# Loads, constants and expert tables moved away from the head of a five-stage kernel

## The reference

```
h = window attention 8x8, 8 heads, rotary positions, on x, then a projection
h = h + local attention over a 7x7 neighbourhood, 8 heads
h = h + feed-forward: relu(Wi h + bi); 2 layers of (shared + one of 16 routed experts + h); Wo
h = h + retention: (q k^T / 8) * 0.99^(i-j) for i >= j, times v, no softmax
h = h + binary experts: sign(x) @ sign(sum of gated weights) * scale, 8 gates
```

## Time and profile before

| | us |
|---|---|
| median of 3 runs | 2014.37 |
| the profiled execution's own time | 2015.21 |
| its span | 2013.4 |
| TensorE busy in the span | 1750.3 (87%) |
| VectorE busy | 1180.1 (59%) |
| ScalarE busy | 973.5 (48%) |
| GpSimd busy | 413.1 (21%) |
| mean granted clock of TensorE | 0.958 |

### The profile page before, as it was taken

The page is one execution under the profiler, slowest core; times in us unless marked ns, Lnnn a source line. Parts: engine busy times, 40 slices in busy tenths (PEclk is TensorE's granted clock), DMA queues, the critical chain, the costliest instruction groups (busy, mean ns, idle before and its releaser), DMA issues.

```text
span 2013.4 us, 94727 instructions
## 1 busy us (share of the span) xinstructions
PE 1750.3 (87%) x35818; PEld 1295.4 (64%) x35818; DVE 1180.1 (59%) x3383; ACT 973.5 (48%) x1765; POOL 413.1 (21%) x474
## 2 busy tenths in 40 slices
PE   1899999966758888888888779999999999999997
PEld 0566666644547777767777557777777777777774
DVE  1456666657724444444444467777777777777762
ACT  0334444423312222222222227777777777777776
POOL 2000000024413233332333222222212222222210
PEclk9799999979878999999999879999999999999998
DMA  3000000114433333434334212333333333333332
GB/s 119 13 12 10 13 13 10 34 33 99 98 89 90 97 97 92 98 96 97 96 93 97 64 37 76 77 77 77 77 78 77 76 78 78 78 78 78 78 77 56
DMA packets 254030, 141.69 MB, mean 70 GB/s; under 512 B 181170, under 2 KB 217906, under 8 KB 253714
## 3 DMA queue, kind: packets, MB, share of 16 engines
q1 hardware_dynamic: 253970, 140.85, 28.3%
HBM read 63.53 MB, written 18.42 MB: 41 GB/s over the span
## 4 chain that ended last, share of the span: by engine, by line
PE 48%; issue 30%; SPq 13%; DVE 4%; ACT 2%; POOL 1%; DMA 1%; DVEq 0%; POOLq 0%; ACTq 0%
PE ps_D L783 12%; PE ps_AV L797 5%; SPq L395 5%; PE ps_D L708 4%; DVE m_sb L1216 2%; SPq L366 2%; PE ps_OT L903 2%; PE ps_J L885 2%; PE ps_OT L866 2%; PE ps_J L830 2%; PE ps_D L704 2%; PE ps_J L857 2%; PE ps_T L876 2%; PE ps_J L911 1%; SPq L384 1%
## 5 line engine op out<-in xcount | busy, mean ns | idle before, releaser
L1035 ACT ACTIVATE prob<-ps_D 128x1024 bf16<-128x1024 f32 x448 | 443.0, 1020 | 98.6 <-PE ps_D L783 98.1
L1216 DVE TENSOR_REDUCE m_sb<-ps_D 128x4 f32<-128x400 f32 x256 | 135.3, 570 | 197.8 <-PE ps_D L686 181.6
L1023 ACT ACTIVATE prob<-ps_D 100x512 f32<-100x512 f32 x256 | 138.8, 594 | 218.4 <-PE ps_D L708 218.4
L474 POOL TENSOR_TENSOR tile_a<-q_st,q_mask 128x1024 f32<-128x1024 f32 x64 | 123.3, 1926 | 400.0 <-DMA q_st<-q_d 348.8
L708 PE MATMUL ps_D<-tile_a,key_patch 64*100 64x128 f32 x2048 | 177.9, 289 | 0.0
L704 PE MATMUL ps_D<-mT,key_rows 64*100 64x128 bf16 x1024 | 129.8, 225 | 51.0 <-ACT mT L1012 32.2
L1170 DVE TENSOR_REDUCE top<-ps_D 128x8 f32<-128x512 f32 x128 | 79.5, 683 | 142.2 <-PE ps_D L562 142.2
L783 PE MATMUL ps_D<-tile_b,w_parts 128*128 128x256 bf16 x1024 | 156.4, 276 | 3.2 <-ACT prob L1035 1.3
L783 PE MATMUL ps_D<-tile_a,w_parts 128*128 128x256 bf16 x1024 | 154.0, 273 | 5.0 <-DVE xg L1315 2.5
L797 PE MATMUL ps_AV<-prob,lane_sum 128*32 128x256 bf16 x2048 | 150.6, 284 | 1.5 <-ACT prob L1035 1.5
L708 PEld LDWEIGHTS ps_D<-tile_a,key_patch 64*100 64x100 f32 x2048 | 147.7, 167 | 0.0
(11 more groups left out here) (172 smaller groups left out, 3911.8 us busy)
## 6 DMA issues: line engine op xcount, KB each, us to landing
tile_b<-v_d SPq DMA_DIRECT2D x640, 40.0 KB
tile_a<-xg SPq DMA_DIRECT2D x384, 64.0 KB, 2.0
tile_b<-xg SPq DMA_DIRECT2D x384, 64.0 KB, 2.0
key_st<-k_d SPq DMA_DIRECT2D x64, 175.0 KB, 3.0
key_st<-k_d SPq DMA_DIRECT2D x64, 167.0 KB, 3.1
w_exp<-experts SPq DMA_DIRECT2D x64, 129.0 KB, 2.3
k_d<-kpad SPq DMA_DIRECT2D x32, 140.0 KB, 2.3
xin<-in_x SPq DMA_DIRECT2D x32, 128.0 KB, 2.2
```

The lines of the kernel that those rows point to most:

```text
L474: gp.tensor_tensor(q_block[:, par, :].rearrange("c (p h q) -> c p h q", h=NH, q=NQ), q_st[:, :].rearrange("c (p a q) -> c p a q", a=1, q=N ...
L1023: act.activation(prob1[0:NKL, 2 * g + x, :], s_loc[x][0:NKL, :], ACT.Exp).then_inc(T2["exp_done"], 1)
L1035: act.activation(sgn[:, k % 4, :], unit(k, par)[:, :], ACT.Sign).then_inc(BN["sign"], 1)
L1216: dve.tensor_reduce(m_sb[:, C * x + HOT[x] + 4 * g:C * x + HOT[x] + 4 * g + 4], m_loc[x][:, 0:4 * NKL].rearrange("p (u n) -> p u n", u=4), ...
```

## The change

The loads are split in two lists. The 12 that the 8x8 stage uses come first, on `s_w`, behind x load 0; the other 31 come on a new semaphore `s_later`, with x loads 1, 2 and 3 behind the 8th, 16th and 24th of them. The fills are put in another order, so that the nine of the 8x8 stage come first. The first waits of TensorE, ScalarE and VectorE are for 12 loads and 9 fills; the waits for all of them stand at the end of the 8x8 stage. The increments of the stages' semaphores are divided: T1 on SyncE (21), T2 and L on GpSimd (35), FF, RT and BN on TensorE (48). GpSimd combines the experts behind its fills. The routes are made by VectorE behind the last `tok_rows`; `spread`, `lane_sum` and the copy of `w_qk3` go to `gate_weights(0)`, and the product for `w_qk3` to the end of local attention on TensorE.

```diff
         def _(sp):
-            loads = [43 pairs]
-            for stage in (T1, T2, L, FF, RT, BN):
-                for signal in stage.values():
-                    sp.sem_inc(signal, 1)
-            for dst, src in loads:
-                sp.dma_start(dst, src).then_inc(s_w, 16)
+            loads = [ident, cos, sin, w_qk, w_qk_swap, w_v1, w_p1, w_p1_rows, b_v1, top_rows, key_shift, head_row]
+            later = [q_mask, ones_h, q_rows, m_sb, decay, decay_q, key_rows 0, key_rows 1, decay_k, w_kq2, w_v2, w_p2, bias2, temp, w_i, b_i,
+                     shared, w_o, b_o, w_qT, w_kT, w_v3, w_gate, b_gate, lane_mask, spread_f, lane_sum_f, w_scale, route_i, keep, experts]
...
+            for signal in T1.values():
+                sp.sem_inc(signal, 1)
+            x_in(0)
+            for dst, src in loads:
+                sp.dma_start(dst, src).then_inc(s_w, 16)
+            for n, (dst, src) in enumerate(later):
+                sp.dma_start(dst, src).then_inc(s_later, 16)
+                if n % 8 == 7 and n < 24:
+                    x_in(n // 8 + 1)
+            with sp.Fori(4, NT) as i:
+                x_in(i)
+
             sp.wait_ge(s_const, NCONST)
-            x_in(0)
-            with sp.Fori(1, NT) as i:
-                x_in(i)
...
         def _(gp):
+            fills = [xT, xT row C, tile_b, top1, ones_32 (5 of them), experts[NEXP], xnp, xn_fg, xn_r (2), kd3, minus_half, zeros, kpad, state, w_parts]
+            for stage in (T2, L):
+                for signal in stage.values():
+                    gp.sem_inc(signal, 1)
...
             gp.wait_ge(s_const, NCONST)
+            gp.wait_ge(s_later, 16 * NLATER)
+            gp.tensor_tensor(shared[:, :, 0:HID], shared[:, :, 0:HID], ident, ALU.add).then_inc(s_shared, 1)
+            gp.wait_ge(s_shared, 1)
+            for l in range(NLAY):
+                if l:
+                    gp.wait_ge(s_prep, l)
+                gp.tensor_tensor(experts[:, l, :, :], experts[:, l, :, :], shared[:, l, :], ALU.add).then_inc(s_prep, 1)
+            gp.wait_ge(s_prep, NLAY)
...
         def _(pe):
-            pe.wait_ge(s_w, 16 * NLOADS)
-            pe.wait_ge(s_const, NCONST)
-            pe.wait_ge(s_prep, 2)
-
-            pe.matmul(bank["AV"][:, C:C + P], w_qT[:, :], w_kT[:, :], start=True, stop=True)
+            for stage in (FF, RT, BN):
+                for signal in stage.values():
+                    pe.sem_inc(signal, 1)
+            pe.wait_ge(s_w, 16 * NFIRST)
+            pe.wait_ge(s_const, NFIRST_CONST)
+
             pe.matmul(bank["AV"][:, 0:C], b_v1[:, :], w_p1[:, :], start=True, stop=True).then_inc(s_bias, 1)
...
             tok_project(NT - 1)
+            pe.wait_ge(s_later, 16 * NLATER)
+            pe.wait_ge(s_const, NCONST)
...
             project(NS - 1)
-            pe.wait_ge(s_placed, 3)
+            pe.matmul(bank["AV"][:, C:C + P], w_qT[:, :], w_kT[:, :], start=True, stop=True).then_inc(s_qk, 1)
...
                 if r is not None:
+                    if isinstance(r, int) and r == 0:
+                        pe.wait_ge(s_qk, 2)
...
                     pe.wait_ge(BN["xs"], times(g + 1))
+                    if isinstance(g, int) and g == 0:
+                        pe.wait_ge(s_placed, 3)
...
         def _(act):
-            act.wait_ge(s_w, 16 * NLOADS)
-            act.wait_ge(s_const, NCONST)
+            act.wait_ge(s_w, 16 * NFIRST)
+            act.wait_ge(s_const, NFIRST_CONST)
...
             pairs(act, tok)
+            act.wait_ge(s_later, 16 * NLATER)
+            act.wait_ge(s_const, NCONST)
...
         def _(dve):
-            dve.wait_ge(s_w, 16 * NLOADS)
-            dve.wait_ge(s_const, NCONST)
-            route_f, shared, experts (2), route_ok (2), route_f, route_x, spread, lane_sum (2)
+            dve.wait_ge(s_w, 16 * NFIRST)
+            dve.wait_ge(s_const, NFIRST_CONST)
             dve.wait_ge(s_bias, 1)
-            dve.tensor_copy(w_qk3[:, :], bank["AV"][:, C:C + P])
             dve.tensor_copy(bias1[:, :], bank["AV"][:, 0:C]).then_inc(s_bias, 1)
             dve.wait_ge(s_bias, 2)
+
+            def routes():
+                dve.wait_ge(s_later, 16 * NLATER)
+                dve.wait_ge(s_const, NCONST)
+                route_f, route_ok (2), route_f, route_x, as before
...
             tok_rows(NT - 1)
+            routes()
...
             def gate_weights(j):
                 if j == 0:
+                    spread, lane_sum (2), as before
+                    dve.wait_ge(s_qk, 1)
+                    dve.tensor_copy(w_qk3[:, :], bank["AV"][:, C:C + P]).then_inc(s_qk, 1)
                     dve.wait_ge(s_gate_w, 16)
```

More of the change, by code:

```diff
@@ L315, in _ @@
         def _(sp):
[L316 to L327, removed]
@@ new lines, in _ @@
+            later = [(q_mask[:, :], a["q_mask"]), (ones_h[:, :, :], a["ones_h"]), (q_rows[:, :], a["q_rows"]), (m_sb[:, :], a["m_init"]),
+                     (decay[:, :], a["decay"]), (decay_q[:, :], a["decay_q"]), (key_rows[:, 0, :], a["key_rows"]),
+                     (key_rows[:, 1, :], a["key_rows"]), (decay_k[:, :], a["decay_k"]), (w_kq2[:, :], a["w_kq2"]), (w_v2[:, :], a["w_v2"]),
+                     (w_p2[:, :, :], a["w_p2"]), (bias2[:, :], a["b_p2"].broadcast_to((P, C))), (temp[:, :], a["temp"].broadcast_to((P, 1))),
+                     (w_i[:, :], a["w_i"]), (b_i[:, :], a["b_i"]), (shared[:, :, :], a["shared"]), (w_o[:, :], a["w_o"]),
+                     (b_o[:, :], a["b_o"].broadcast_to((P, C))), (w_qT[:, :], a["w_qT"]), (w_kT[:, :], a["w_kT"]), (w_v3[:, :], a["w_v3"]),
+                     (w_gate[:, :], a["w_gate"]), (b_gate[:, :], a["b_gate"]), (lane_mask[:, :], a["lane_mask"]), (spread_f[:, :], a["spread"]),
+                     (lane_sum_f[:, :], a["lane_sum"]), (w_scale[:, :], a["w_scale"]), (route_i[:, :], a["route"]), (keep[:, :, :], a["keep"]),
+                     (experts[:, :, 0:NEXP, :], a["experts"])]
@@ L335, in x_in @@
+            assert len(loads) == NFIRST and len(later) == NLATER
             def x_in(i):
@@ L451, in _ @@
             gp.wait_ge(s_const, NCONST)
+            gp.wait_ge(s_later, 16 * NLATER)
+            gp.tensor_tensor(shared[:, :, 0:HID], shared[:, :, 0:HID],
+                             ident[:, :].rearrange("p (a n) -> p a n", a=1).broadcast_to((P, NLAY, P)), ALU.add).then_inc(s_shared, 1)
+            gp.wait_ge(s_shared, 1)
+            for l in range(NLAY):
+                if l:
+                    gp.wait_ge(s_prep, l)
+                gp.tensor_tensor(experts[:, l, :, :], experts[:, l, :, :],
+                                 shared[:, l, :].rearrange("p (a n) -> p a n", a=1).broadcast_to((P, NEXP + 1, HID + 1)), ALU.add).then_inc(s_prep, 1)
+            gp.wait_ge(s_prep, NLAY)
             def patches(buf):
@@ L1120, in _ @@
-            for l in range(NLAY):
-                dve.tensor_tensor(experts[:, l, :, :], experts[:, l, :, :],
-                                  shared[:, l, :].rearrange("p (a n) -> p a n", a=1).broadcast_to((P, NEXP + 1, HID + 1)), ALU.add).then_inc(s_prep, 1)
-            dve.tensor_scalar(route_ok[:, :], route_i[:, :], 0.0, None, ALU.is_ge).then_inc(s_route, 1)
-            dve.wait_ge(s_route, 2)
-            dve.scalar_tensor_tensor(out=route_ok[:, :], in0=route_i[:, :], scalar=float(NEXP), in1=route_ok[:, :], op0=ALU.is_lt, op1=ALU.mult).then_inc(s_route, 1)
```

44 lines of the change are left out of this document (24 added, 20 removed).

## The result

The changed kernel took 1995.78 us (median of 6 runs, 1984.85 to 2001.62) against 2015.84 for the kernel before beside it: a ratio of 0.9896, interval 0.9863 to 0.9928. That is 20 us gained where 31 were forecast, 12 us above the predicted time and outside the range. Over every run of this study the kernel before has a mean of 2015.8 us (79 runs) and the changed one 1994.7 (14): a gain of 21. So 1.4 us of the miss is that the three runs shown for before lay low; about 10 us want a cause.

The account below looks back on a forecast made before the run. Bound: nothing computed for 41.5 us, while TensorE waits for 43 loads issued behind 104 SyncE increments and for VectorE's expert combination. Sum: 2015.21 - 31.9 + 1.0 = 1984.3, median 0.84 lower: 1983.5 us; range 1975 to 1992.

Parts of the forecast that it names:

- The start: Head of the kernel: TensorE's first turning of x at 11.3 us instead of 43.2, 31.9 us earlier.
- The opening: First tiles of the 8x8 stage: their 15.7 us over the steady pace was left unchanged.
- Rival (a): Opening tiles: loads and GpSimd's work shift a gap, the clock falls otherwise; 1968 or 1994.5 us; chance 0.15.
- Cost nothing: 8x8 stage: later loads, with the experts' behind x load 3, delay nothing; 0 us.
- The bound that I gave: 8x8 stage: without a tile's time as cover, one turn would wait up to 8.9 us behind the experts' load.
- The increments: Engine heads: SyncE's 104 spread over four engines, all before 10.3 us; TensorE's 48 take 3.1 us, done by 4.
- GpSimd's layers: Experts' combination on GpSimd during the 8x8 stage: 4.1 us for each of two layers, between 2.4 and 6.2.
- The lock: 8x8 stage: GpSimd's second layer holds VectorE's `rot` 1.0 us, inside 1.15 us of slack; taken as 0, at most 4.1.
- rival (b): 8x8 stage: both GpSimd layers catch a `rot`, each holding it 5.0 us; 1993.5 us; chance 0.07.
- The routes: VectorE between the last tile's rows and the next stage's moments: five moved instructions add 1.0 us, between 0.8 and 1.3.
- The base: Whole kernel before: starting time of the sum, 2015.21 us in the profiled execution, the runs' median 0.84 lower.

Follow-up runs that it names:

- delayed kernel: Changed kernel with 26 dummy semaphore increments on TensorE ahead of the first turning: 1999.93 us, ratio 0.9923.
- late version: Changed kernel with the experts' load issued behind x load 15 instead of x load 3, GpSimd's combination following it: 2001.29 us, ratio 0.9923.
- joined kernel: Changed kernel, 48 increments moved from TensorE to SyncE plus 32 extra instructions, experts' load behind last x load, GpSimd's layers behind `rot` of tiles 30, 31: 1990.94 us.
- new sort: The changed kernel and the variants built on it, as opposed to the kernel before; the changed kernel itself has a mean of 1994.7 us.
- increments moved: Changed kernel with TensorE's 48 increments moved to SyncE ahead of its fills wait, 32 extra instructions behind them: 1991.0, 1988.73 and 1990.18 us.
- stage_end: Changed kernel with 80 extra SyncE increments, experts' load behind the last x load, GpSimd's layers behind `rot` of tiles 30 and 31: 1994.42 us, ratio 0.9902.

## Why the prediction was wrong

- **The start**, -31.9: right, measured -31.87 at the turning; every step on its path within 0.2 us (GpSimd's fills, off the path, began at 3.45 and not at 2.8). By the first scores 1.1 us were gone: the product for the keys (L562 of the changed kernel) took 2.05 us there instead of 1.10. The low clock would fit that length, but the granted clock reads 1.00 from 11 to 29 us, so the cause is not shown.
- **The opening**: this step failed. "The new opening has the same instructions in the same order from the turning on, so I leave the loss as it is." The instructions were the same, but not where they stand in the program nor when they arrive from memory. Tiles 0 to 5 took 72.6 us instead of 68.0, 4.5 more. The same sentence left the loss behind tile 5 at nothing, and there it was 4.0 more, with no cause shown. Rival (a) said nearly this (the loads shift a gap and the clock falls otherwise) and had 0.15; it should have had more, since my own rows 5 and 12 showed 15.7 us hanging on gaps. Its 1994.5 is close to the 1995.78 by luck: it priced two tiles at 11 us, and the opening lost 4.5.
- **"Cost nothing"** for the experts' load behind x load 3: I looked for who waits for an x load, and nobody does. The one who waited was TensorE, in a gap of 4.2 to 4.8 us in the four profiles, beside a late block of the instruction queue. The bound that I gave (a turn waits up to 8.9 us) was of the right sort for the wrong waiter. Of the opening's loss this is the part in tile 2; on the whole time its removal had no effect that the runs can tell.
- **The increments**: "TensorE's 48 take 3.1 us and are done by 4" took SyncE's price. In the delayed kernel 26 took 4.1 us on TensorE; at that price the 48 take some 7.5 us, an estimate, and are done by about 8, still ahead of 10.16. What the forecast missed is what they do to the rest: the runs without them at TensorE's head are about 4 us faster, and SyncE's 83 fewer shift two stages by -5.1 and +6.6, a term put at nothing without a reason.
- **GpSimd's layers**: 4.5 us each (9.04 for two), between my 4.1 from rows and the 4.8 that I estimated from the Trainium skill (GPSIMD Engine Reference, "3.1 Elementwise"). The lock held `rot` for 0.25 us, not 1.0, and cost nothing, as taken; the price of rival (b) is real, as the 4.59 us of the late version shows.
- **The routes**, +1.0: right. The changed kernel's VectorE between the last rows of h and the next moments:

```profile
405.81 0.42 DVE L1170 TENSOR_TENSOR h<-ps_OT,bias 128x256 f32<-128x256 f32 x1 [1.41 <-PE ps_OT L636]
406.15 0.17 DVE L1149 CAST route_f<-route_i 1x64 f32<-1x64 int32 x1
...
406.95 0.18 DVE L1156 TENSOR_SCALAR route_x<-route_f 1x64 int32<-1x64 f32 x1
407.06 0.59 DVE L1114 BATCH_NORM_STATS2 stats_pre<-h 128x6 f32<-128x64 f32 x4
```

  They fill 0.9 us, and the passage is 1.8 us longer; the other 0.9 has no cause shown (in the joined kernel the passage is only 0.9 longer).
- **The base**: 2014.37 from three runs stood for 2015.8. That is 1.4 us of the miss.
- **The account of the 10 us**: about 4 go with the increments at TensorE's head. Putting SyncE's loops back changed the whole time by nothing that the runs can tell (1994.6 against 1994.7), and so did moving the load. The other 5 to 6 have no cause shown: even the joined kernel's mean is 5 above the forecast corrected for the base.
- **Open.** Tile 5 to tile 31 takes 281.0 to 287.0 us in the profiles of before and 283.8 to 291.8 in those of the new sort. Each tile of 13.9 us there has a stretch of 6.8 us at a granted clock of 0.50 and costs 3.1, and one of 12.4 has half of both; there are none to two in before and one to three in after. The waits of a steady tile are the same. Neither the moment of the start, the load, SyncE's place nor TensorE's place removes it in every profile; nothing tried here tells chance from cause. Open too is why more time lies outside the span in many executions of after (1.8 to 3.8 us, 2.6 in the mean of 14; in before 1.8, with few exceptions and 2.6 at most); with the increments moved and joined all 12 runs have 1.8. That every extra microsecond at the start moves the end by as much was not tested beyond the delay of 4.

## What to carry to other kernels

Work taken off the head of a kernel is worth its full length only if what follows arrives unchanged, and a program's instructions are among what must arrive: read the instruction queue's row and TensorE's "issue" gaps where loops run for the first time, and keep megabyte loads out of there if another place costs nothing (here it shortened the tiles, and the whole not measurably). Semaphore increments and other small instructions at the head of an engine's program also move every loop behind them; put them where the engine idles and a loop's place stays, and compare the length of stages that were not touched. Let GpSimd's long two-input instructions on SBUF tiles wait until VectorE is past its own instruction on two SBUF tiles.

## What the runs showed of the hardware

- A block of instructions (16 KB, one every 6 us in the opening) came 2 to 4 us late during a load of 2064 KB; TensorE's stop there grew from 1.4 us to 3.6 in the kernel before, and was 3.3 to 4.8 in the changed kernel and its variants with the load in that place.
- A loop of SyncE that issues 14 DMAs took 8.69, 8.77, 8.81 or 8.89 us for the same instructions, repeatable within 0.01 for one program, with 40 to 83 instructions more or less ahead of it.
- Runs with 48 semaphore increments at the head of TensorE have a mean 4.4 us higher than runs without (2.0 either way, on different chips) and a standard deviation of 4.7 instead of 1.9; the four runs of stage_end, with the increments, spread by only 0.8.
- 26 semaphore increments took 4.1 us on TensorE, 0.16 each; on SyncE the first load is issued at 1.96 us with 21 ahead of it and at 7.29 with 104, 0.064 each.
- An addition of two SBUF tiles on VectorE took 4.59 us instead of 0.69 beside a two-input addition of SBUF tiles on GpSimd of 4.5 us.
